# A graph layer on one core: blocks of nodes by number modulo 98, two slot tables instead of three, scores in passes of four chunks while the tables fill, q split to bf16 once

## The reference, cut to what matters

```python
h = maximum(layernorm(x), 0)                     # [12500, 128]
hn, q, k, v = h @ Wn + bn, h @ Wq + bq, h @ Wk + bk, h @ Wv + bv
eh = edge_attr_64 @ We + be                      # [412500, 128]
hmid = leaky_relu(concat([q[src], k[dst], eh]) @ A1 + b1, 0.2)
scores = leaky_relu(hmid @ A2 + b2, 0.2)         # [412500, 8]
w = softmax(scores.mean(-1), axis=0)             # over all edges
out = segment_sum(w[:, None] * v[dst], src, 12500)
y = hn + out
return x + gamma * (y - mean(y)) / sqrt(var(y) + 1e-5) + beta
```

## Time and profile before

| what | us |
|---|---|
| median of 3 runs (lowest, highest) | 7358.18 (7349.99, 7363.12) |
| span of the profiled execution | 5836.5 |
| median less span | 1521.7 |
| first scatter issued | 148.2 |
| last scatter issued | 4235.2 |
| stage C, first to last `mid` | 4255.4 to 4834.7 |
| stage D, first product to end | 4844.3 to 5836.5 |

### The profile page before, as it was taken

One profiled execution on the slowest core, in us unless ns is written; L12 is line 12 of the kernel. 1 busy time (PEld: TensorE's weight loads), 2 busy tenths in 40 slices (PEclk: granted clock), 3 DMA queues, 4 the chain that ended last, 5 costly groups with the idle time before them and its releaser, 6 DMA issues. The chain is left out here.

```text
span 5836.5 us, 160082 instructions
## 1 busy us (share of the span) xinstructions
PE 5234.9 (90%) x42668; PEld 4250.7 (73%) x43061; DVE 4377.7 (75%) x11683; ACT 3010.9 (52%) x6881; POOL 3193.7 (55%) x3405
## 2 busy tenths in 40 slices
PE   7988888887998999999899999999589999999999
PEld 4877777786666666666666666666467778989998
DVE  7544444445888888888788888888389998888888
ACT  5433333333554555555455555555234447888887
POOL 2777777777777777777777777777700000000000
PEclk9999999999999999999999999999789999999999
DMA  7776766765788888876766666676366668999999
GB/s 214 220 223 228 222 205 237 240 205 163 240 264 261 255 263 260 263 227 203 208 207 205 204 205 206 203 209 199 127 152 169 170 169 225 263 265 263 264 264 244
DMA packets 1852626, 1285.46 MB, mean 220 GB/s; under 512 B 627828, under 2 KB 1708784, under 8 KB 1852451
## 3 DMA queue, kind: packets, MB, share of 16 engines
q1 hardware_dynamic: 1683633, 828.13, 54.0%
q0 software_dynamic: 154752, 449.19, 20.8%
q10 hardware_dynamic: 14066, 6.41, 0.4%
HBM read 668.25 MB, written 621.46 MB: 221 GB/s over the span
## 5 line engine op out<-in xcount | busy, mean ns | idle before, releaser
L1151 POOL DMA_INDIRECT slots<-rows,slot_i x3224 | 3105.9, 963 | 997.1 <-issue 957.8
L1206 PE MATMUL ps_row<-win,mixed 128*128 128x256 f32 x6448 | 1695.5, 392 | 236.5 <-ACT rows L1304 235.2
L1206 PEld LDWEIGHTS ps_row<-win,mixed 128*128 128x128 f32 x6448 | 1165.8, 194 | 413.9 <-ACT rows L1304 218.1
L1304 ACT ACTIVATE rows<-ps_row 128x512 f32<-128x512 f32 x1612 | 945.9, 597 | 536.0 <-PE ps_row L1206 515.9
L896 ACT ACTIVATE low<-ps_z 128x512 f32<-128x512 f32 x931 | 553.6, 595 | 1008.0 <-PE ps_z L762 791.9
L1976 PE MATMUL ps_y<-v_rows,spot 128*128 128x128 f32 x7448 | 948.4, 283 | 41.2 <-ACT spot L2125 18.1
L1976 PEld LDWEIGHTS ps_y<-v_rows,spot 128*128 128x128 f32 x7448 | 888.4, 192 | 101.1 <-issue 72.9
L2307 DVE TENSOR_SCALAR spot<-iota_f,v_rows,weight 128x128 f32<-128x128 f32 x2744 | 783.9, 347 | 121.9 <-PE ps_y L1976 112.7
L921 DVE TENSOR_TENSOR mid<-low,ps_z 128x512 f32<-128x512 f32 x931 | 635.5, 683 | 233.6 <-ACT low L896 233.1
L912 DVE TENSOR_SCALAR onehot<-ps_lo,part 128x512 bf16<-128x512 f32 x931 | 694.0, 745 | 92.5 <-PE ps_lo L740 87.8
L762 PE MATMUL ps_z<-onehot,q_bits 128*128 128x512 bf16 (+1 forms) x2547 | 690.1, 376 | 26.2 <-DVE onehot L912 3.0
(11 more groups left out here) (178 smaller groups left out, 5902.9 us busy)
## 6 DMA issues: line engine op xcount, KB each, us to landing
u_rows<-slots SPq DMA_DIRECT2D x931, 258.0 KB, 3.2
v_rows<-slots SPq DMA_DIRECT2D x784, 258.0 KB, 3.7
edges<-edge_attr_dram SPq DMA_DIRECT2D x403, 256.0 KB
slots<-no_row SPq DMA_DIRECT2D x194, 408.0 KB
slots<-no_row SPq DMA_DIRECT2D x106, 544.0 KB
slots<-rows,slot_i POOLq DMA_INDIRECT x3224
v_rows<-slots SPq DMA_DIRECT2D x196, 193.5 KB, 3.5
win<-kv_tab SPq DMA_DIRECT2D x403, 64.0 KB
```

Of the source, the lines that this page charges most:

```text
L1151: pool.indirect_dma_start(slots_tab[h], bass.IndirectOffsetOnAxis(slot_i[:, u, j:j + 1], 0), rows[:, u, j, :], None).then_inc(scattered[u] ...
L1206: last = pe.matmul(ps_row[:, k % 2, j % 2, :], mixed[:, u % 2, j, :], win[:, u, :], start=True, stop=True)
L1304: nc.scalar.activation(rows[:, u, 2 * k:2 * k + 2, 0:2 * U0].rearrange("p j (a c) -> p j a c", a=2)[:, :, :, 0:D], ps_row[:, k % 2, :, :]. ...
```

## The change

Nodes go to blocks by number modulo 98: block b holds nodes b, 98+b, 196+b and so on, and the local number is the quotient. Tables in DRAM keep the order of the node numbers, and a block is read with a stride of 98 rows, in two DMAs (partitions 0 to 111, and the rest). Two slot tables of 16 and 20 chunks a block take the place of three (36 chunks instead of 38); the first takes groups 0 to 177. A row has 264 floats instead of 272.

A unit is now four chunks of one block, and units go in nine passes: pass p is one unit of every block. Passes 0 to 6 (686 units) run inside stage B, while the table they read is still filling: before a pass SP waits until so many groups are written that each block should hold the slots, and DVE compares the counts (`check_pass`). Stage B has two units a group from group 76 on (loop bodies of 4 groups) and three a group in groups 368 to 399 (`quick`, bodies of 8 groups), then two again. Stage C has 196 units, with rings of six. Groups 12 to 60 also split q (`prep_step`), two blocks a group, into `qb_tab` (bf16, three parts); `load_unit` then brings 96 KB of it with every unit, and the chain of four operations is gone. In stage D a block has 9 units of 4 chunks, BUNCH is 3 and the ring is 9.

```diff
-PARTS = (12, 12, 14)
-FILLED = (9, 9, 10)
-CUTS = (126, 254)
+CAPS = (16 * P, 20 * P)
+FILLED = (13, 16)
+CUT = 178
+DONE = 7
+EARLY = 68
+START = 76
+PREP = 12
+AHEAD = 8
+QUICK = 368
+BODY = 8
+LEFT_BODY = 12
+LEFT_RING = 6
-BUNCH = 2
+BUNCH = 3
-RING = 9
-LAST_RING = 7
+RING = 8
-    RW = 272
+    RW = 264
...
+                    nc.gpsimd.memset(x_sb[P - 32:P, WIDE:NT, :], 0.0).then_inc(pad_made, 1)
...
+        def load_unit(sp, o, r, b, p, freed):
+            if freed is not None:
+                sp.wait_ge(o.z_ready, freed)
+                sp.sem_inc(passed, 1)
+            h, row = place_of(p, b)
+            sp.dma_start(o.u_rows[:, r, :, :],
+                         slots_tab[h][bass.ds(row, UNIT * P), :].rearrange("(c p) f -> p c f", p=P)[:, :, D:D + U0]).then_inc(o.u_in[r], 16)
+            sp.dma_start(o.q_bits[:, r, :], qb_tab[bass.ds(b * P, P), :]).then_inc(o.u_in[r], 16)
...
-            nc.scalar.activation(o.q_bits[:, b, 0, :], o.q_rows[:, b, :], ACT.Copy).then_inc(o.q_chain, 1)
...
-                    def both(s, u, i, units):
...
+                    def both(s, u, units):
+                        v, more, late = (u + 1) % UNROLL, in_group(s, 1), len(units) // 2
+                        if more:
+                            turn_half(s + 1, v, 0)
+                        make_rows(s, u, 0)
+                        unit(*units[0])
+                        make_rows(s, u, 1)
+                        for n in units[1:late]:
+                            unit(*n)
+                        if more:
+                            turn_half(s + 1, v, 1)
+                        make_rows(s, u, 2)
+                        for n in units[late:]:
+                            unit(*n)
+                        if more:
+                            rank(s + 1, v)
+                        make_rows(s, u, 3)
...
+                    def wait_pass(p):
+                        seen = CUT if p == MASKED else HELD_UP[p] + 1
+                        for u in range(UNROLL):
+                            sp.wait_ge(scattered[u], 16 * PER * ((seen + UNROLL - 1 - u) // UNROLL))
...
-                        looped(pe, UNROLL, BOTH - 2, warm_step)
+                        looped(pe, UNROLL, START - UNROLL, warm_step)
...
-            VRING = 10
+            VRING = 9
```

More of the change, by code:

```diff
@@ L801, in q_turn @@
-        def q_turn(o, i, k, late):
-            for n in range(1, BLOCKS + 1):
-                first = -(-(n - 1) * o.part // UNIT)
-                if k == first + late and has_unit(o, i, n * o.part // UNIT):
-                    return i + n // BLOCKS, n % BLOCKS
-            return None
-        def q_on_act(act, o, i, k):
-            if q_turn(o, i, k, 0):
-                q_top(act, o, *q_turn(o, i, k, 0))
-            if q_turn(o, i, k, 1):
-                q_middle(act, o, *q_turn(o, i, k, 1))
@@ L1011, in body @@
-            def body(i, step):
-                for j in range(EIGHT):
-                    units = tuple(k for k in units_of(j) if has_unit(o, i, k))
-                    if units:
-                        step(i * EIGHT + (BOTH + j), (BOTH + j) % UNROLL, i, units)
-            def body_loop(eng, first, end, step):
-                with eng.Fori(first, end) as i:
-                    body(i, step)
+            NQ = NT // 2
+            STEADY = (QUICK - START) // UNROLL
+            LAST_BODY = bodies(o) - 1
@@ new lines, in staged, with bits_of, split_here, steady @@
+            def staged(u):
+                return o.u_rows[:, u, :, :].rearrange("p c f -> p (c f)")[:, 0:2 * D].rearrange("p (t f) -> p t f", t=2)
+            def bits_of(u, m):
+                return o.q_bits[:, 2 * u:2 * u + 2, m * D:(m + 1) * D]
+            def split_here(s, late):
+                return (not known(s)) or 0 <= s - PREP - late < NQ
+            def steady(eng, first, end, step):
+                with eng.Fori(first, end) as i:
+                    for j in range(UNROLL):
+                        step(i * UNROLL + (START + j), j, [(i, 2 * j), (i, 2 * j + 1)])
@@ new lines, in quick, with one_body, last_body @@
+            def quick(eng, step):
+                with eng.Fori(0, FAST) as i:
+                    for j in range(EIGHT):
+                        units = [unit_of(o, i * 3 + STEADY, 3 * j + n) for n in range(3)]
+                        step(i * EIGHT + (QUICK + j), j % UNROLL, units)
+            def one_body(i, step):
+                for j in range(UNROLL):
+                    step(i * UNROLL + START + j, j, [(i, 2 * j), (i, 2 * j + 1)])
+            def last_body(step):
+                for j in range(3):
+                    step(LOOPS_END + j, j, [(LAST_BODY, 2 * j), (LAST_BODY, 2 * j + 1)])
@@ L1951, in _, with heads_of @@
             def _(pe):
+                def heads_of(i, k):
+                    for m in range(batch_size(o, i, k)):
+                        last = heads(pe, o, i, k // BATCH * BATCH + m)
+                    return last
                 def score_step(i, k):
@@ L1956, in score_step @@
                     if ended(o, i, k - 2):
-                        j, end = ended(o, i, k - 2)
-                        first, size = o.batches[batch_of(o, end)]
-                        for m in range(size):
-                            heads(pe, o, j, first + m)
+                        heads_of(*ended(o, i, k - 2))
                     if has_unit(o, i, k + 1):
```

1045 lines of the change are left out of this document (509 added, 536 removed).

## The result

The changed kernel takes 7132.8 us (median of four runs, 7125.7 to 7139.1), the kernel before 7360.7 beside it (7350.0 to 7367.3). The ratio is 0.9689, 95% interval 0.9669 to 0.9709: 228 us less. The forecast was 7101, its range 7045 to 7175. So the sum came out near. The picture of stage B that it rests on did not, and that is the larger part of what follows.

The account below looks back on a forecast made before the run. The prediction took POOL's scatters to bound stage B and PE to bound C and D. From the median 7358 us, +40 in B, -245 in C and -52 in D gave 7101 us, range 7045 to 7175.

Parts of the forecast that it names:

- POOL paces stage B, anything under 10.1 us a group is free: Stage B: POOL's scatters set the pace; PE, DVE or ACT work costs nothing while PE averages under 10.1 us a group.
- scatters 1.26 us apart until group 368: Stage B, sign: POOL's scatters stay 1.26 us from start to start until group 368; earlier gaps would make the prediction wrong.
- ScalarE wait once for a free row buffer in the groups of two: Stage B, sign: ACT should wait for free buffers in the part with two units a group.
- +40 for the 32 groups of three, 0 for the others: Stage B: three-unit groups cost 54 us plus 10 for body entries less 24 of PE's lead; extra units elsewhere cost nothing.
- The term for one group of three: Stage B: a three-unit group takes 11.8 us, 1.7 over POOL, 54 us in all.
- the wait that I had priced at 1.4 us once a group: Stage B, three-unit groups: PE waits for ACT and DVE to make `mid` between adjacent units, 1.4 us.
- Stage C, -245: Stage C: 147 units fewer at 1.67 us each, 245 us less.
- Loads of q and the ring of six: Stage C: 96 KB more per unit and six buffers instead of seven cost nothing; 8.3 us stays for a landing.
- Stage D, -52, up to +50 back: Stage D: 196 chunks fewer at 0.266 us each, 52 us less; load delays cost 0, up to +50.
- The rival of late loads: Stages C or D: shallower rings and one more DMA a unit delay loads; 49 us in D, 7150 us, chance 0.15.
- PE takes over B, slower than before: Stage B, rival: slower-clocked PE exceeds 10.1 us in two-unit groups; decides from 11.1, 7486 us at 11.5; chance 0.04.
- The shorter scatter: Stage B, rival: scatter time falls with the row's bytes, 2.9% less, B shrinks by 120 us; 6981 us, chance 0.03.

Follow-up runs that it names:

- apart: Changed kernel with the units of each three-unit group taken in the earlier kernel's order, row work between any two; 7177.6 us against 7429.6, ratio 0.9669.
- base: The kernel before the change, run once more unchanged for a trace whose own time is known; 7415.7 us.
- fewer_pairs: Changed kernel with 8 groups of three units instead of 32, units in them separated by row work, scatters released in twos; 6897.2 us, ratio 0.9357.

## Why the prediction was right, and where it was wrong

**POOL paces stage B, anything under 10.1 us a group is free: wrong.** It was read correctly from a trace that is no picture of the runs that are timed. The warning stood in the numbers: 1521.7 us of the time had no place in the trace. I took them as outside the span and unchanged. They are 3.8 us in each of 403 groups, and how many there are depends on the order and the releases in a group. The sign I had named, scatters 1.26 us apart until group 368, failed from the first groups on: the first gap of over 1 us stands at 167 us. Nor did ScalarE wait once for a free row buffer in the groups of two, as I had expected.

**"+40 for the 32 groups of three, 0 for the others": the sum of B near, its terms not.** From the table: three units 32 x (19.96 - 13.73) = +199; 64 groups that had no units, 64 x 0.70 = +45; 262 groups that had 2.25 units on the average and lose the quarter, 262 x (13.73 - 14.61) = -230, the old third units above all; -5 for the rest. That is +9 between the traces, about +70 by the runs. The term for one group of three was 1.7 us over POOL's pace; it measured 6.2 over a group of two. For the wait that I had priced at 1.4 us once a group, for `mid` between units side by side, these are TensorE's waits in the 32 groups (total, times, longest), of the changed kernel and of apart:

```profile
PE ps_s L755 <- DVE mid L833: 199.1, 28, 8.0
...
PE ps_s L755 <- DVE mid L833: 142.0, 34, 7.2
```

That is 7.1 us a time, five times the price, and still 4.2 where no unit stands beside another, so it is not that chain alone.
The order adds 1.6 to 2.2 us of the 6.2. The release in fours, for which I had no term, adds 2.4 to 3.1 more. Holds stand behind both, and how much of the 6.2 us is theirs is not shown.

**Stage C, -245: right.** -255.6 with its start; (6167.5 - 5842.3) / 195 = 1.67 us a unit. Loads of q and the ring of six cost nothing: the loads of q land in 3.2 us at the median and 4.9 at most.

**Stage D, -52, up to +50 back: right, 10 short.** -42.3. From the groups of D in the changed kernel:

```profile
L2017 PE MATMUL ps_y<-v_rows,spot 128*128 128x128 f32 x7032 | 867.1, 281 | 71.8 <-ACT spot L2158 60.6 <-DVE spot L2328 11.0
...
L2328 DVE TENSOR_SCALAR spot<-iota_f,v_rows,weight 128x128 f32<-128x128 f32 x2628 | 744.7, 350 | 57.3 <-DMA v_rows<-slots 32.0 <-issue 13.2 <-PE ps_y L2017 4.8
```

VectorE now waits 32.0 us for `v_rows`, which stood in no group of the earlier trace rows, and TensorE 60.6 us for ScalarE's part of `spot`, 18.1 there. The rival of late loads was real at a fifth of its price.

**The rival "PE takes over B, slower than before".** Half of it happened: POOL lost the pace, and the clock in B is 0.85. But POOL had lost it before the change too, so it did not decide the sign. The shorter scatter is refuted: 960 ns at the median, as before.

**Staying in the range** was partly luck: of B's parts I had 40 for the groups of three, which took 199, and nothing for the others, which gave back some 190 between the traces. The two errors nearly cancelled.

## What to carry to other kernels

Compare the span of a profile with the time of its own run before reading anything else. If a fifth is missing, the trace can't say what paces the kernel: take a second one. Price work that moves under a "free" cover by the measured time of a group with and without it, in a trace that agrees with the runs. And when the number of pieces between two releases to another engine changes, choose the order and the grain of the releases anew: here two edits of a few lines were worth as much as the whole change.

## What the runs showed of the hardware that I had not expected

While GpSimd issues indirect DMAs one after another, work that waits for a TensorE product can stay held, 8.1 us at most in base and 9.5 in the changed kernel, although the product is over by the profile. A sixth to a quarter of these waits end while a scatter runs, the others behind one; at the median it is 1.5 us behind the end of a scatter. Counted over the units of stage B of base, ScalarE began `low` more than 1 us after everything that it needed in 242 of the 492 units whose product ended inside a burst (the 0.30 us behind a scatter counted to it), and in 2 of the 96 others; with releases in twos (fewer_pairs) 302 of 492 and 1 of 170; in the trace shown of before none of 588, all inside its one long burst. VectorE's `mid` came 0.03 us after ScalarE's `low`, or after VectorE was free, in all units of base between 1500 and 4100 us.

Of the three engines only TensorE's signals are late, as the updates above show, and the work of the others takes no longer: `low` is 597 ns at the median inside and outside the bursts. The ends of products are modelled in the profile. But the five products of the hold shown began one after another over 2.6 us, and their updates came within 0.26 us, so the earlier ones at least were over before. What keeps the signal back, a write of the product or the signal's own way, can't be told. SyncE is touched too: in B of the changed kernel 798 of its 9182 register and semaphore instructions took over 0.5 us, in the trace shown of before 132 of 8628.

Open stays what holds them, and what was different in the execution of the trace shown, in which the same program had hardly any of it (in 22 common stands of 64 us in all in stage B, where base has 151 of 472 us). SyncE's read of a register and TensorE's load in groups without units were ruled out, and the distance of GpSimd from its rows up to 7 to 15 us. Whether the issuing on GpSimd or the transfers do it is not separated: the packets of a scatter go on behind its instruction, and the common stands of the changed kernel end 0.4 us at the median behind the last packet of a scatter, 1.2 behind the last instruction. Nor is it known whether the recording takes a part: the profile has 585 updates for the 588 `low` of the trace shown, and 440 for 581 in base (1900 to 5700 us). A kernel with half the scatters wasn't tried, since it would read slots that nothing had filled.
